# Scaling the last residual branches on ScalarE, and two pieces of VectorE work moved ahead

## The reference

```python
q = (x @ Wq).reshape(B, L, H, d);  feat = elu(q) + 1
KV = einsum('nshd,nshv->nhdv', feat, q / L)
Z  = 1.0 / (einsum('nlhd,nhd->nlh', feat, feat.sum(1)) + 1e-6)
msg = (einsum('nlhd,nhdv,nlh->nlhv', feat, KV, Z) * L).reshape(B, L, D) @ Wm
x = x + layernorm(msg, g1, b1)                  # branch 1
x = x + layernorm(relu(msg @ W1) @ W2, g2, b2)  # branch 2
# around it: h = layernorm(x)*(1+ca)+sa;  x = x + ga * attn(h)
h = layernorm(x) * (1 + cb) + sb
probs = softmax(h @ Wg)                # 8 experts per token
# top-k (512) tokens of each expert over all tokens, an expert for each token,
out[token] = x + gb * weight * gelu(h @ W1[e]) @ W2[e]
```

## Time and profile before

| | |
|---|---|
| median of 3 runs | 236.51 us (235.86 to 236.67) |
| the profiled execution, own time | 237.87 us |
| its span | 236.1 us |
| PE busy | 182.1 us (77%) |
| DVE busy | 176.5 us (75%) |
| ACT busy | 132.2 us (56%) |
| POOL busy | 150.8 us (64%) |

### The profile page before, as it was taken

The page is one execution under the profiler, slowest core; times in us unless marked ns, Lnnn a source line. Parts: engine busy times, 40 slices in busy tenths (PEclk is TensorE's granted clock), DMA queues, the critical chain, the costliest instruction groups (busy, mean ns, idle before and its releaser), DMA issues.

```text
span 236.1 us, 4343 instructions
## 1 busy us (share of the span) xinstructions
PE 182.1 (77%) x1161; PEld 143.4 (61%) x1161; DVE 176.5 (75%) x661; ACT 132.2 (56%) x425; POOL 150.8 (64%) x236
## 2 busy tenths in 40 slices
PE   0878988999799999947386779996679989998000
PEld 0635767878569988846234265664468879997000
DVE  1889989999995899999888988899204998555100
ACT  2159984366646889952987873324425766874000
POOL 8698836457563566664399990027777777777771
PEclk9999999999979999975557555999979999999955
DMA  5895000000010000000056334003333332111110
GB/s 174 254 293 171 0 3 1 0 3 0 2 47 0 0 4 0 1 3 0 0 170 190 89 89 133 3 0 90 96 104 114 99 106 101 58 44 60 55 45 22
DMA packets 16968, 15.49 MB, mean 66 GB/s; under 512 B 1905, under 2 KB 14321, under 8 KB 16945
## 3 DMA queue, kind: packets, MB, share of 16 engines
q1 hardware_dynamic: 14288, 9.70, 13.7%
q0 software_dynamic: 2240, 5.51, 7.6%
q10 hardware_dynamic: 416, 0.01, 0.1%
HBM read 8.92 MB, written 6.29 MB: 64 GB/s over the span
## 4 chain that ended last, share of the span: by engine, by line
PE 44%; DVE 32%; ACT 7%; issue 7%; POOL 5%; DMA 2%; POOLq 1%; DVEq 0%; ACTq 0%
PE pH L974 7%; DVE scr L1309 6%; PE pQ L983 6%; PE pQ L881 5%; POOL out_dram L422 4%; PE pH L804 3%; PE pQ L815 3%; DVE t L1134 3%; DVE x_sb L1190 3%; PE pH L871 2%; DVE rows L1030 2%; DVE bn L1022 2%; DVE x_sb L1136 2%; DVE t L1132 2%; PE pQ L796 2%
## 5 line engine op out<-in xcount | busy, mean ns | idle before, releaser
L419 POOL DMA_INDIRECT rows<-table_dram,gidx x28 | 28.9, 1032 | 24.9 <-DVE gidx L1401 16.7
L422 POOL DMA_INDIRECT out_dram<-rows,gidx x28 | 27.6, 986 | 8.5 <-issue 5.8
L974 PE MATMUL pH<-x_sb,hid 128*128 (+1 forms) x140 | 22.5, 283 | 1.1 <-ACT hid L637 0.9
L983 PE MATMUL pQ<-ew,u 128*128 (+1 forms) x140 | 22.2, 281 | 1.2 <-ACT u L651 0.8
L983 PEld LDWEIGHTS pQ<-ew,u 128*128 128x128 f32 x140 | 18.4, 191 | 3.1 <-issue 1.9
L651 ACT ACTIVATE u<-pH 128x256 f32<-128x256 f32 x35 | 13.4, 383 | 11.5 <-PE pH L974 11.4
L974 PEld LDWEIGHTS pH<-x_sb,hid 128*128 128x128 f32 x140 | 18.4, 191 | 2.2 <-issue 2.0
L1450 DVE SCALAR_TENSOR_TENSOR t<-pQ,wslot,scr 128x128 f32<-128x128 f32 x35 | 12.2, 348 | 10.0 <-PE pQ L983 9.7
L524 ACT ACTIVATE sqj<-pQ 128x128 bf16<-128x128 f32 x60 | 15.8, 283 | 6.6 <-PE pQ L796 3.3
L287 POOL TENSOR_TENSOR yr<-yv,neghalf 128x4 f32<-128x4 f32 x16 | 17.0, 1064 | 1.3
L373 POOL TENSOR_TENSOR scr<-feat,z 128x512 f32<-128x512 f32 x8 | 9.6, 1203 | 12.6 <-DVE z L1167 12.6
(11 more groups left out here) (331 smaller groups left out, 539.7 us busy)
## 6 DMA issues: line engine op xcount, KB each, us to landing
table_dram<-x_sb SPq DMA_DIRECT2D x9, 256.0 KB, 2.8
x_sb<-in_L_attn_x_dram SPq DMA_DIRECT2D x8, 256.0 KB, 5.2
table_dram<-rows SPq DMA_DIRECT2D x7, 256.0 KB, 2.4
ew<-in_L_ffn_W_dram SPq DMA_DIRECT2D x2, 512.0 KB, 9.2
w1d<-in_L_ffn_W_dram SPq DMA_DIRECT2D x1, 1024.0 KB, 11.6
rows<-table_dram,gidx POOLq DMA_INDIRECT x28, 2.8
out_dram<-rows,gidx POOLq DMA_INDIRECT x28
wmod_sb<-in_L_wmod_dram SPq DMA_DIRECT2D x1, 384.0 KB, 4.6
```

The lines of the kernel that those rows point to most:

```text
L419: gp.indirect_dma_start(row[:, t, :], None, table[:, :], bass.IndirectOffsetOnAxis(gidx[:, t:t + 1], 0)).then_inc(gathered[t], 16)
L422: gp.indirect_dma_start(out.rearrange("b l d -> (b l) d"), bass.IndirectOffsetOnAxis(gidx[:, t:t + 1], 0), row[:, t, D:2 * D], None).then_ ...
L974: mm = te.matmul(pH[i % 2][:, f * P:(f + 1) * P], wcur[:, i % RW, f * P:(f + 1) * P], xt[:, bass.ds(i - e, 1), :], start=True, stop=True)
L983: mm = te.matmul(pQ[i % 2][:, 0:D], eh[:, i % 2, f * P:(f + 1) * P], ew[:, bass.ds(e, 1), f * D:(f + 1) * D], start=(f == 0), stop=(f == 1))
```

## The change: what it does

Three edits, all at the second pass. (1) For three of the last four branches (group 6's two and group 7's first) ACT multiplies `u` by `yr` in place, one ACTIVATE with a scale pointer for each tile (`a_scaled`, 12 instructions, placed behind the squares of group 7 and ahead of the rows of group 4), and DVE adds each branch to x with one 128x512 addition (`v_x1_scaled`). Group 7's second branch stays as it was. (2) DVE's `v_acc` of group 7 is done whole in step 5 and not spread over steps 7 to 9; `v_u2` of group 7 goes ahead of the additions of group 6, and `v_stats3` of group 6 ahead of those of group 7. (3) `v_logits(0)` moves from step 9 to the end of step 8.

```diff
+            def a_scaled(g, k):
+                act.wait_ge(S[("u1_done", "u2_done")[k]], g + 1)
+                act.wait_ge(S[("yr1_done", "yr2_done")[k]], g + 1)
+                u = (u1[:, g % 3], u2[:, g % 2])[k]
+                for t in range(GT):
+                    last = act.activation(u[:, t, :], u[:, t, :], ACT.Identity, scale=yr[:, g % RY, k * GT + t:k * GT + t + 1])
+                last.then_inc(S["scaled"], 1)
...
                 if s == G + 2:
                     a_square(s - 3, 1, "y2_ready", "sq2")
+                    a_scaled(G - 2, 0)
+                    a_scaled(G - 2, 1)
+                    a_scaled(G - 1, 0)
                 if 0 <= s - 6 < ACT_ROWS:
                     a_xn3(s - 6)
...
+            def v_x1_scaled(g):
+                x1 = bgroup(x_sb, g)
+                dve.wait_ge(S["scaled"], 2 * (g - G + 2) + 1)
+                link(dve.tensor_tensor(x1, x1, u1[:, g % 3], ALU.add))
+                if g == G - 2:
+                    dve.wait_ge(S["scaled"], 2)
+                    dve.tensor_tensor(x1, x1, u2[:, g % 2], ALU.add).then_inc(S["x1_done"], 1)
+                else:
+                    dve.wait_ge(S["yr2_done"], g + 1)
+                    for t in range(GT):
+                        x1 = x_sb[:, g * GT + t, :]
+                        last = dve.scalar_tensor_tensor(x1, u2[:, g % 2, t, :], yr[:, g % RY, GT + t:GT + t + 1], x1, ALU.mult, ALU.add)
+                    last.then_inc(S["x1_done"], 1)
...
-                if s == G + 1:
-                    v_logits(0)
                 if s == G + 2:
                     v_probs(0)
-                if 0 <= s - 4 < G:
+                if s == G + 2:
+                    v_u2(G - 1)
+                if 0 <= s - 4 < G - 2:
                     v_x1(s - 4)
+                elif 0 <= s - 4 < G:
+                    v_x1_scaled(s - 4)
+                if s == G + 2:
+                    v_stats3(G - 2)
...
-                if G - 1 <= s < G + 2:
-                    v_acc_step(G - 1, s - G + 1)
-                if 0 <= s - 3 < G:
+                if s == GB + 1:
+                    v_acc(G - 1)
+                if s == G:
+                    v_logits(0)
+                if 0 <= s - 3 < G - 1:
                     v_u2(s - 3)
```

More of the change, by code:

```diff
@@ L185, in build @@
             ks_done gts_done kv_ready kvt_done mall_ready mall_done
-            den_ready z_done qp_done tq qT_done y1_ready m1_ready relu0 y2_ready sq1 sq2 u1_done u2_done yr1_done yr2_done x1_done
+            den_ready z_done qp_done tq qT_done y1_ready m1_ready relu0 y2_ready sq1 sq2 u1_done u2_done yr1_done yr2_done scaled x1_done
             wgs_done cm_ready wgc_done stats3 rs3 nm_done xn3 tx3 h2_done txd h2_last lg_ready
@@ L1285, in be_ @@
                 return t[:, :, :].unsqueeze(3).to_broadcast([P, B, E, TB])
-            v_stats3(G - 2)
             v_stats3(G - 1)
```

## The result

The changed kernel takes 237.50 us (median of 5 runs, 237.03 to 237.87), the kernel before, on the same chip, 236.35 (235.86 to 236.67): ratio 1.0051, 95% interval 1.0032 to 1.0070. That is 1.2 us more (0.8 to 1.7). The forecast was 237.4.

A forecast was written before the change was run, and what follows sets the result against it. The prediction took the chain of waits at the second pass's end as the bound: ACT's queue makes group 6's copy 0.88 us late, the moved pieces add nothing, so 236.51 + 0.88 = 237.4 us, range 236.0 to 238.6.

The forecast's parts named there:

- ACT's price and queue: End of second pass: twelve ACTIVATEs 0.295 us apart, 3.54 us in all, make group 6's copy on ACT 0.88 us late.
- the slack: Time ACT has to spare ahead of group 6's copy, from 104.00 to 106.56: 2.56 us.
- DVE's additions wait, and don't decide: Group 6's second addition waits for the eighth ACTIVATE; its x is 0.2 us later, still before ACT is free.
- Group 7's saving: The 1.5 us or so that DVE saves for group 7 come to nothing, since PE takes it only at 109.96.
- The moved pieces: `v_acc` (some 2.05 us) hidden in step 5's 2.57 us DVE wait, 0.4 to spare; batch 0's logits (1.27) hidden in step 8.
- Price on the chain: nothing, gain: nothing: Moved DVE work costs the chain nothing; of nearly 2 us gained at most 1.1 is real, and ACT's scaling takes it back.
- The relay: Copies, routings and transposes of groups 6 and 7 up to the search: no slack, so 0.88 us goes through.
- the prediction's own signs of being wrong: ACT idle before group 6's copy, a pitch other than 0.29, or a granted clock other than 0.50 over 104 to 113 us.
- Absolute times: Places in the changed profile, such as the search's start at 116.9 us and not 116.0.
- The size: The whole loss, from ACT's queue at the end of the second pass: 0.88 us.
- Everything to the end hangs on it in order: From the search, at about 116 us, to the end: what is late at group 6's copy is as late at the end.

The follow-up runs named there:

- e2: The changed kernel with ACT's rows of group 4 moved from ahead of group 6's copy to behind it; 236.67 us, ratio 1.0000 to the kernel before.
- e4: The changed kernel without scaling on ACT: DVE does all products, in the changed order; 236.64 us, ratio 1.0006 to the kernel before.
- e3: The kernel before plus twelve spare ACTIVATEs on ACT in the place of the change's, results never read; 237.35 us, ratio 1.0063.
- e6: The kernel before plus eight spare ACTIVATEs on ACT, for group 6's two branches only; 236.67 us, ratio 1.0012.
- e1: The kernel before with `v_acc` of group 7 whole in step 5 and batch 0's logits in step 8, old order, no ACT scaling; 235.93 us, ratio 0.9982.
- e5: The kernel before with only `v_acc` of group 7 moved whole to step 5; 236.63 us, ratio 0.9994.
- e7: e1 with group 6's first branch added a step earlier, in step 9, all on DVE; 234.40 us, ratio 0.9924 to the kernel before.
- e8: e7 with four scalings on ACT (group 7's first branch) and the rows of group 4 behind group 6's copy; 234.52 us, ratio 0.9926 to the kernel before.

## Why the prediction was right, and where it was off

- **ACT's price and queue: right.** The pitch was put at 0.295 from the neighbouring form and is 0.292; the copy was to be late by 0.88 and is late by 0.94, with no idle time before it. (The two count from different points: the 0.88 has the squares 0.1 sooner, so it is 0.98 behind the squares, where 0.94 was measured. In e2 and e4, at the clock of before, the squares start 0.17 and 0.16 sooner.) e3 and e6 show the queue as the cause from both sides of the slack. The Trainium skill (ScalarE: Activation LUTs, What ACT_TABLE_LOAD costs) gives an ACTIVATE without pointers 186 ns + 0.833 ns per element, 93 ns more for a pointer operand and 93 ns of overlap between neighbours: an estimate of 293 ns from start to start here. The trace agrees, with 0.292 us.
- **DVE's additions wait, and don't decide: right.** Group 6's sum ends at 104.1, 4.3 us behind the squares against 3.9 before. The prediction had it 0.2 late; e2, where nothing hides it, has the tail 0.34 late.
- **Group 7's saving is worth nothing: right.** The 1.67 us of idle time before its logits show it.
- **The moved pieces: hidden at one clock and not at the other.** The prediction read the room in step 5, 2.57 us, from an execution whose clock was 0.57 over 66 to 70 us. At that clock it holds: e4, with the same move, still has 0.59 us of idle time before `u` (0.4 forecast). At full clock there is less room. e3 is the kernel before in this place, and `u` waits only 0.89 us there:

```profile
72.72 0.69 DVE L1184 TENSOR_TENSOR u<-pQ,rC 128x512 f32<-128x512 f32 x1 [0.89 <-ACT sqj L524]
```

  In the changed kernel the three pieces fill 71.80 to 73.97, and `u` starts at 73.97, 1.25 us later. Most of that is caught up a step later, where `u` waits 0.87 us for ACT in e3 (79.73) and not at all in after (80.02). Group 6's squares on ACT start at 97.73 and not at 97.48, and since the profile of after is 0.05 behind already at 65 us, 0.2 us is left. It lies ahead of the tail.
- **"Price on the chain: nothing, gain: nothing": wrong taken by itself.** The prediction put the gain that is real at 1.1 us, and e1's transpose comes 1.02 sooner. It also said that the change takes it back, which is so, but laid all of it on ACT, since "ACT's scaling can't start before 102.4". e4 shows that the early `u` of group 7 alone takes it back (1.2 us at the transpose, e4 against e1); ACT's scaling comes on top (0.74 in the tail, the changed kernel against e4). The sum is the same.
- **The relay: right, with one row off.** It passes the delay on, 0.94 at the copy and 0.93 at the search. Only the transpose that opens it ran at full clock (0.66, against 1.12 forecast), since the granted clock fell a little later: 0.86 over 104 to 105 us and not 0.50. It was off the path by then, with the copy waiting for ACT. The routings took 1.88, as forecast. One of the prediction's own signs of being wrong came true by this: the granted clock over 104 to 113 us was 0.54 and not 0.50. It changed nothing for the changed kernel, but it does for the kernel before (next but one).
- **Absolute times: off.** The search was to start at 116.9 and started at 115.36, since the profile lay 1.57 us ahead by the squares. Behind the squares it is 15.5 forecast (116.88 - 101.35) and 15.48 measured.
- **The size: too small by a quarter, and the clock is a likely reason.** From group 6's transpose to the search it is 10.34 us in e1, e5 and e7 alike, whether group 6's routing takes 1.16, 1.47 or 1.06 us: there DVE's queue decides. In the profile of before it is 10.59, and DVE waits for PE at the end, which it doesn't in e7. The last logits before, then in e7, and then group 6's transpose in e3:

```profile
112.61 0.19 DVE L1215 TENSOR_TENSOR m<-pQ,rs 128x32 f32<-128x32 f32 x1 [0.16 <-PE pQ L834]
```

```profile
108.79 0.18 DVE L1217 TENSOR_TENSOR m<-pQ,rs 128x32 f32<-128x32 f32 x1
```

```profile
103.72 0.66 PE L832 MATMUL pT<-ident,x_sb 128*128 128x128 f32 x4 [3.20 <-DVE x_sb L1198]
```

  e3 is the kernel before as far as this transpose: it stands 3.96 us behind the squares as there, but takes 0.66 us and not 1.12. So the kernel before has executions at full clock too, and its tail in them is 3.96 + 10.34 = 14.30 us by an estimate from these rows, not 14.55; no profile shows one. Held against 14.30, the change loses 1.18 us, e3 loses 1.17, and e1, e5 and e7 gain 1.02, 0.76 and 1.97. All of these lie inside the intervals of the ratios; e5's 1.01 against 14.55 doesn't. The slack shrinks likewise: the search follows the copy by 9.43 us (15.48 - 6.05), so the copy may stand 14.30 - 9.43 = 4.87 us behind the squares, and ACT is free for it at 2.55: 2.3 us and not 2.56, just what eight operations take.
- **The median: hit in part by luck.** The change cost 237.50 - 236.35 = 1.15 us by the medians, and 0.88 was forecast. The forecast started from 236.51, 0.16 above the 236.35 of the kernel before in the comparison, and so came within 0.1 of 237.50.
- **"Everything to the end hangs on it in order": nearly.** From the search to POOL's last store it is 114.24 us before and 114.17 to 114.34 in e2 to e8, so that in these profiles the tail's difference arrives whole. It is 114.64 in the changed kernel and 115.49 in e1, where the whole gain is gone again at the end. By the ratios the change costs 1.2 us (0.8 to 1.7) and e3 1.5 (0.8 to 2.2); e1 and e5 gain 0.4 and 0.1, e7 1.8 (1.0 to 2.5).

**What stays open** is what e1 and the changed kernel lose behind the search. The last stretch is POOL's queue: 28 gathers, then 28 stores, 0.30 us apart. First gather, first store and last store, before:

```profile
157.94 1.47 POOL L419 DMA_INDIRECT rows<-table_dram,gidx  x1 [16.70 <-DVE gidx L1401]
...
195.37 1.09 POOL L422 DMA_INDIRECT out_dram<-rows,gidx  x1 [0.31 <-issue]
...
230.24 0.97 POOL L422 DMA_INDIRECT out_dram<-rows,gidx  x1 [0.30 <-issue]
```

and after:

```profile
156.81 1.46 POOL L419 DMA_INDIRECT rows<-table_dram,gidx  x1 [16.17 <-DVE gidx L1431]
...
195.39 1.01 POOL L422 DMA_INDIRECT out_dram<-rows,gidx  x1 [0.30 <-DVE rows L1488]
...
230.00 0.97 POOL L422 DMA_INDIRECT out_dram<-rows,gidx  x1 [0.30 <-issue]
```

The gathers of after start 1.13 us sooner, and its stores at the same time. The gathers take 37.4 us in the profiles of before, e2, e4, e5 and e6, and 38.4 to 38.6 in those of the changed kernel, e1, e3, e7 and e8, each of which has one gather of 1.68 or 1.69 us that the others lack. The second kind start by 156.81 us, the first kind from 157.48 on. But long gathers don't by themselves take a gain back: e7 and e8 have them, and their gains arrive, since the stretch ahead of them, from the search to the first gather, is 0.6 us shorter than before (41.3 against 41.9). In e1 it isn't (42.2). No run here changes this overlap alone, so why gathers get longer, and why only e1 pays for it in full, is not shown.

## What to carry to other kernels

An idle engine's room is not its idle share but the time from where the new work would start to where its next needed instruction is due, less what stands between in its queue: in the profile of before 2.56 us, worth eight of these operations and not twelve. Work that is moved to relieve a busy engine should go into a wait of that same engine first (e7: four products into 0.86 us of idle time, 0.76% faster, 0.44 to 1.07); and an instruction put forward that waits for something late holds back everything behind it (e4). Compare two profiles by the stretch between events, never by their spans, when the granted clock parts them, and read idle time in executions at both clocks before filling it: the room in step 5 was 2.57 us in one and 0.89 in the other.

## What the runs showed of the hardware that was not expected

- The granted clock of the same stretch, with PE equally busy, differs from execution to execution: 66 to 70 us at 0.57 or 0.58 in five of the ten profiles (before, e2, e4, e5, e6), at 0.62 in e8 and at 1.00 in the rest (the changed kernel, e1, e3, e7). e3 is the kernel before up to group 7's squares, and has them at 99.76 against 101.45.
- How soon the clock falls in the tail changes what a gap costs. Over 104 to 105 us it was 1.00 in e1, e3, e5, e7 and e8, 0.86 in the changed kernel and 0.50 in before, e2, e4 and e6. Where group 6's transpose comes early (e7, 101.83), group 6's routing takes 1.06 us and not 1.88. Yet those 0.82 us are no part of e7's gain of 2.22: from transpose to search e7 takes the same 10.34 us as e5, whose routing takes 1.47.
- An indirect gather's issue on POOL mostly takes 0.95 us, from a certain point on 1.02 to 1.04 (from 186.91 us before, 182.82 after), and single ones 1.45 to 1.69. The experts' sums on DVE aren't the cause by themselves: before, they begin at 182.05 (L1458), and the gathers at 183.16, 184.42 and 185.66 still take 0.94 or 0.95.
